# SwitchHead attention: scores with the keys in four partition groups, probabilities turned by VectorE instead of TensorE, row maxima combined through DRAM

## What is computed

```python
def _gate(x, Wsel):                       # sigmoid scores, all but the best two of eight set to zero
    ...
q = _rope(jnp.einsum('bsd,hdp->bhsp', x, Wq))
k = _rope(jnp.einsum('bsd,hdp->bhsp', x, Wk))
v = jnp.einsum('bsd,bhse,hedp->bhsp', x, _gate(x, Wsel_v), Wv)
att = jax.nn.softmax(jnp.einsum('bhsp,bhtp->bhst', q, k) / np.sqrt(P), axis=-1)
o = jnp.einsum('bhst,bhtp->bhsp', att, v)
return jnp.einsum('bhsp,bhse,hepd->bsd', o, _gate(x, Wsel_o), Wo)
```

## Time and profile before

| | |
|---|---|
| runs | 5350.47, 5362.56, 5364.59 us (median 5362.56) |
| the profiled execution | 5350.9 us, of which the span of the trace is 5349.1 us |
| the stage of SwitchHead's loop | 1057 to 3644 us, 2587 us, 256 tiles |
| TensorE in that stage | 2551.35 us busy, granted clock 1.00 |
| VectorE, ScalarE, GpSimd there | 1520.72, 1338.64, 1157.34 us busy |
| DMA there | 0.31 of 16 engines, 81 GB/s |

### The profile page before, as it was taken

How to read it: one execution, slowest core, us unless ns; L and a number is a source line. 1 busy time by engine, 2 the same in 40 slices (tenths; PEclk the granted TensorE clock), 3 DMA queues, 4 the chain that set the end, 5 groups by cost and what they waited for, 6 DMA issues and landing times.

```text
span 5349.1 us, 83763 instructions
## 1 busy us (share of the span) xinstructions
PE 4801.0 (90%) x30340; PEld 2480.0 (46%) x30378; DVE 3571.9 (67%) x4077; ACT 2898.9 (54%) x3797; POOL 2348.7 (44%) x1499
## 2 busy tenths in 40 slices
PE   6989898689999999999999999997888988888856
PEld 2334333256556666565666556564333322222226
DVE  5899999866655565556655674654776778888721
ACT  5665556245445545555455554553555557667743
POOL 4888888535534543535534444443221221120014
PEclk8999999899999999999999999998999999999978
DMA  4555555323332332333323332233112101101005
GB/s 152 189 182 183 179 190 193 124 56 82 86 80 78 86 94 72 82 83 79 94 68 86 89 95 65 72 91 85 39 34 43 41 25 26 25 25 25 2 30 169
DMA packets 202377, 467.59 MB, mean 87 GB/s; under 512 B 35179, under 2 KB 52078, under 8 KB 201316
## 3 DMA queue, kind: packets, MB, share of 16 engines
q1 hardware_dynamic: 198968, 455.89, 29.9%
q0 software_dynamic: 3008, 6.32, 0.3%
HBM read 417.51 MB, written 33.99 MB: 84 GB/s over the span
## 4 chain that ended last, share of the span: by engine, by line
PE 72%; issue 9%; DVE 8%; ACT 6%; POOL 3%; DMA 0%; SPq 0%; POOLq 0%; DVEq 0%; ACTq 0%
PE ps L2258 8%; PE ps L1350 8%; PE ps L1370 8%; PE ps L1389 8%; PE ps L1358 7%; PE ps L1339 7%; PE ps L548 4%; PE ps L2229 3%; PE ps L2211 3%; ACT n_P L2293 3%; PE ps L495 2%; PE ps L1332 2%; DVE ps L713 1%; DVE n_MX L2372 1%; DVE m_HH L734 1%
## 5 line engine op out<-in xcount | busy, mean ns | idle before, releaser
L2372 DVE TENSOR_REDUCE n_MX<-ps 128x2 f32<-128x1024 f32 (+6 forms) x1034 | 982.2, 979 | 235.6 <-PE ps L2211 137.1
L1496 ACT ACTIVATE s_P<-ps,s_MX 128x1024 f32<-128x1024 f32 x512 | 570.4, 1114 | 968.1 <-DVE s_MX L1660 968.0
L2293 ACT ACTIVATE n_P<-ps 128x1024 f32<-128x1024 f32 (+4 forms) x1022 | 825.3, 838 | 447.2 <-PE ps L2229 233.7
L1652 DVE TENSOR_TENSOR XTB<-ps,s_GVJ 128x1024 f32<-128x1024 f32 x256 | 313.2, 1223 | 837.3 <-PE ps L1339 836.4
L771 POOL TENSOR_TENSOR m_PR<-m_HH,m_CS 128x1024 f32<-128x1024 f32 x256 | 605.9, 2381 | 156.2 <-issue 129.4
L1660 DVE TENSOR_REDUCE s_MX<-ps 128x1 f32<-128x1024 f32 x512 | 600.3, 1214 | 32.1 <-PE ps L1350 32.0
L1867 POOL TENSOR_TENSOR s_OG<-s_OG,s_OT 128x1024 f32<-128x1024 f32 x256 | 604.4, 2374 | 38.8 <-DMA s_OG<-s_gt 38.6
L1505 ACT ACTIVATE shared<-ps 128x1024 f32<-128x1024 f32 x512 | 496.7, 1023 | 140.0 <-PE ps L1358 138.4
L1350 PE MATMUL ps<-s_QF 64*128 64x512 f32 x2048 | 510.6, 617 | 28.1 <-POOL s_QF L1859 20.0
L1358 PEld LDWEIGHTS ps<-ident,s_P 128*128 128x128 f32 x4096 | 464.0, 141 | 150.5 <-issue 135.3
L1370 PEld LDWEIGHTS ps<-shared,s_V 128*64 128x64 f32 x8192 | 442.0, 137 | 197.4 <-issue 172.4
(11 more groups left out here) (352 smaller groups left out, 6484.7 us busy)
## 6 DMA issues: line engine op xcount, KB each, us to landing
m_CS<-m_rows_c SPq DMA_DIRECT2D x256, 512.0 KB
s_OG<-s_gt SPq DMA_DIRECT2D x512, 256.0 KB, 4.2
m_BS<-m_rows_c SPq DMA_DIRECT2D x80, 512.0 KB
s_WV<-in_s_v SPq DMA_DIRECT2D x32, 512.0 KB, 4.0
s_TA<-XTB SPq DMA_DIRECT2D x256, 64.0 KB, 2.3
s_WO<-in_s_o SPq DMA_DIRECT2D x32, 512.0 KB, 5.3
g_WB<-in_g_wx SPq DMA_DIRECT2D x23, 578.0 KB
n_parts<-n_PT SPq DMA_DIRECT2D x14, 768.0 KB, 3.4
```

The costliest lines, as they stand in the source:

```text
L2293: ins = s.activation(P[:, at:at + x.shape[1], lo:512], x[:, :, lo:512], ACT.Exp, scale=scale)
L2372: ins = v.tensor_reduce(self.MX[:, q, at:at + x.shape[1], hp, t], x[:, :, 0:width], AX.X, ALU.max)
```

## The change

- `row`: the same products in 32 small matmuls per tile instead of 4. Each takes 32 queries (a), one quarter of the keys (x: of every 128 keys, 32) and one head (h), and writes 32 partitions x 256 columns. The scores of a query now lie in four groups of 32 partitions. ScalarE only copies them to P (`row`).
- `turn`: VectorE transposes P in blocks of 32 x 32 from SBUF to SBUF, one instruction of 128 x 1024 per head. TensorE's 16 transposes and ScalarE's two copies of them are gone. `values` reads PT in another pattern, with the same number and size of matmuls.
- the maximum: VectorE reduces each head of P to four columns (`max`), SyncE writes these 128 x 8 values to DRAM (`max`) and reads them back as 32 x 4 x 8 (`join`); VectorE reduces over the four (`most`), SyncE writes the 32 x 8 result four times (`most`) and reads it back on 128 partitions (`bias`). ScalarE's exponential then runs in place on P, in four pieces of 256 columns per head (`exp`).
- the sums go the same way once per four tiles: write, read (`gather`), reduce, reciprocal and a 32 x 32 transpose on VectorE, write (`spread`), two reads that broadcast over 64 partitions each (`over`). TensorE's four transposes, ScalarE's copy and GpSimd's spreading are gone.
- `v`: the sum over the 8 experts moves from VectorE's one reduction to three additions on GpSimd, of 512, 256 and 128 elements.
- `swap`: the four DMAs of `qk` are issued in the turn after it.
- the order inside `turn`, and six buffers of P instead of four.

```diff
-    NP = 4
+    NP = 6
...
+        k, half = m % 4, lambda late: self.of_half((m - late) // 4)
+        if due(1):
+            out.append(("most", *tile(1)))
         if due(2):
-            g = m - 2
-            out.append(("values", *self.pair(g // 8), g % 8))
-            if g % 4 == 3:
-                out.extend([("keep", *self.of_half(g // 4)), ("sums", *self.of_half(g // 4))])
+            out.append(("turn", *tile(2), 1))
+        if k == 1 and due(5):
+            out.append(("sums", *half(5)))
+        if k == 2 and due(6):
+            out.append(("over", *half(6)))
+        if due(1):
+            out.append(("bias", *tile(1)))
+        if k == 1 and due(5):
+            out.append(("gather", *half(5)))
+        if d in (3, 5) and b < NB and m // 8 + 1 < 8 * NB:
+            out.append(("swap", *self.pair(m // 8 + 1), d // 2 - 1))
         if m < 7:
             next(ahead)
         if due(self.GATED):
@@ -969,18 +989,33 @@
         if due(self.GATED + 1):
             h, e = part(self.GATED + 1)
             out.append(("onto", *self.of_half(h), e))
-            if e == 3:
-                out.append(("collect", *self.of_half(h)))
+        if due(0):
+            out.append(("max", *tile(0)))
+        for _ in range(2 if m == 2 else 1):
+            next(vs, None)
+        if due(1):
+            out.extend([("exp", *tile(1), 0), ("exp", *tile(1), 1)])
+        if k == 1 and due(5):
+            out.append(("recip", *half(5)))
+        if due(1):
+            out.append(("turn", *tile(1), 0))
+        if due(0):
+            out.append(("join", *tile(0)))
+        if k == 1 and due(5):
+            out.append(("spread", *half(5)))
+        if k == 2 and due(6):
+            out.append(("scale", *half(6)))
+        if due(self.GATED + 1) and part(self.GATED + 1)[1] == 3:
+            out.append(("collect", *self.of_half(part(self.GATED + 1)[0])))
+        if due(2):
+            g = m - 2
+            out.append(("values", *self.pair(g // 8), g % 8))
+            if g % 4 == 3:
+                out.append(("keep", *self.of_half(g // 4)))
         if d in (3, 5) and b < NB and m // 8 + 1 < 8 * NB:
             out.append(("rope", *self.pair(m // 8 + 1), d // 2 - 1))
-        next(turns, None)
-        next(turns, None)
         if m < N:
             next(ahead, None)
-        if m % 4 == 0 and due(4):
-            out.append(("recip", *self.of_half(m // 4 - 1)))
-        for _ in range(2 if m == 2 else 1):
-            next(vs, None)
...
+            elif kind == "max":
+                g = self.tile(*step[1:])
+                sp.wait_ge(self.mx_done, g + 1)
+                if g > 1:
+                    sp.wait_ge(self.mg_in, 16 * (g - 1))
+                sp.dma_start(self.mx_d[g % 2], self.MX[:, g % 2, :]).then_inc(self.mx_out, 16)
+            elif kind == "join":
+                g = self.tile(*step[1:])
+                sp.wait_ge(self.mx_out, 16 * (g + 1))
+                if g > 1:
+                    sp.wait_ge(self.most_done, g - 1)
+                sp.dma_start(self.MG[:, g % 2, :, :], self.mx_d[g % 2].rearrange("(x p) e -> p x e", x=4)).then_inc(self.mg_in, 16)
+            elif kind == "most":
+                g = self.tile(*step[1:])
+                sp.wait_ge(self.most_done, g + 1)
+                if g > 1:
+                    sp.wait_ge(self.mb_in, 16 * (g - 1))
+                sp.dma_start(self.mr_d[g % 2].rearrange("(x p) e -> p x e", x=4),
+                             self.MR[:, g % 2, :].unsqueeze(1).to_broadcast([32, 4, 8])).then_inc(self.mr_out, 16)
+            elif kind == "bias":
+                g = self.tile(*step[1:])
+                sp.wait_ge(self.mr_out, 16 * (g + 1))
+                if g > 1:
+                    sp.wait_ge(self.exp_done, 2 * (g - 1))
+                sp.dma_start(self.MB[:, g % 2, :], self.mr_d[g % 2]).then_inc(self.mb_in, 16)
+            elif kind == "sums":
+                k = self.half(*step[1:])
+                sp.wait_ge(self.exp_done, 8 * (k + 1))
+                if k > 1:
+                    sp.wait_ge(self.su_in, 16 * (k - 1))
+                sp.dma_start(self.su_d[k % 2], self.SU[:, k % 2, :]).then_inc(self.su_out, 16)
...
+                rows = self.sums_d[k % 2].rearrange("(t h a) q -> h t (a q)", t=4, h=2)
+                for h in range(2):
+                    sp.dma_start(self.OR[k % 2][64 * h:64 * h + 64, 1, :].rearrange("p (t n) -> p t n", t=4),
+                                 rows[h].partition_broadcast(64)).then_inc(self.or_in, 16)
...
-            elif kind == "qk":
-                k = n(*step)
+            elif kind == "swap":
+                k = n("qk", *step[1:])
                 sp.wait_ge(self.raw_done, k)
                 if k > 1:
                     sp.wait_ge(self.rope_done, k - 1)
...
-                for q in chunks(L):
-                    for h in range(2):
-                        hs = slice(64 * h, 64 * h + 64)
-                        ins = pe.matmul(r.ap(two[h])[:, q], QF[hs, 0, t * 128:(t + 1) * 128], QF[hs, 1, q], start=True, stop=True)
-                        if q.stop == L:
...
+                for a in range(4):
+                    for x in range(4):
+                        for h in range(2):
+                            hs, at = slice(64 * h, 64 * h + 64), 128 * t + 32 * a
+                            keys = QF[hs, 1, :].rearrange("p (k x n) -> p k x n", x=4, n=32)[:, :, x, :]
+                            place = r.ap(two[h])[32 * x:32 * x + 32, 256 * a:256 * a + 256]
+                            ins = pe.matmul(place.rearrange("p (k n) -> p k n", n=32), QF[hs, 0, at:at + 32], keys,
+                                            start=True, stop=True)
+                            if a == x == 3:
...
+                        place = self.O[64 * h:64 * h + 64, 128 * (g % 4):128 * (g % 4) + 128].rearrange("p (a n) -> p a n", n=32)
+                        P = self.PT[g % 2][:, h, :].rearrange("p (a k n) -> p a k n", a=4, n=32)[:, :, i, :]
+                        ins = pe.matmul(place, self.V[j % 2][:, h, i, :], P, start=i == 0, stop=i == NT - 1)
...
-                    s.wait_ge(self.values_done, g - 1)
-                s.activation(self.PT[g % 2][:, step[4], :, :].rearrange("p k n -> p (k n)"), ps, ACT.Copy).then_inc(*r.take(step))
+                    s.wait_ge(self.pt_done, x - self.NP + 1)
+                s.activation(self.P[x % self.NP][:, :], ps, ACT.Copy).then_inc(*r.take(step))
...
+            elif kind == "exp":
+                g, x, h = self.tile(*step[1:4]), self.head(step), step[4]
+                if h == 0:
+                    s.wait_ge(self.mb_in, 16 * (g + 1))
+                    if g % 4 == 0 and g >= 8:
+                        s.wait_ge(self.su_out, 16 * (g // 4 - 1))
+                for a in range(4):
+                    P, at = self.P[x % self.NP][:, 256 * a:256 * a + 256], 8 * (g % 4) + 4 * h + a
+                    ins = s.activation(P, P, ACT.Exp, bias=self.MB[:, g % 2, 4 * h + a:4 * h + a + 1],
+                                       accum_out=self.SU[:, g // 4 % 2, at:at + 1])
...
-                r.taken(v, step)
-                v.tensor_reduce(self.V[u][:, :, t, :], four(self.VP), AX.X, ALU.add).then_inc(self.v_done, 1)
-            elif kind == "row":
-                x = self.head(step)
-                r.filled(v, step)
-                if x >= 8:
-                    r.taken(v, self.old("row", x - 8))
-                v.tensor_reduce(self.MX[:, x % 8:x % 8 + 1], ps, AX.X, ALU.max, negate=True).then_inc(self.mx_done, 1)
+            elif kind == "max":
+                g = self.tile(*step[1:])
+                if g > 1:
+                    v.wait_ge(self.mx_out, 16 * (g - 1))
+                for h in range(2):
+                    x = self.head((*step, h))
+                    r.taken(v, ("row", *step[1:], h))
+                    ins = v.tensor_reduce(self.MX[:, g % 2, 4 * h:4 * h + 4],
+                                          self.P[x % self.NP][:, :].rearrange("p (a k) -> p a k", a=4), AX.X, ALU.max)
+                ins.then_inc(self.mx_done, 1)
+            elif kind == "most":
+                g = self.tile(*step[1:])
+                v.wait_ge(self.mg_in, 16 * (g + 1))
+                if g > 1:
+                    v.wait_ge(self.mr_out, 16 * (g - 1))
+                v.tensor_reduce(self.MR[:, g % 2, :], self.MG[:, g % 2, :, :].rearrange("p x e -> p e x"), AX.X, ALU.max,
+                                negate=True).then_inc(self.most_done, 1)
+            elif kind == "turn":
+                g, x = self.tile(*step[1:4]), self.head(step)
+                v.wait_ge(self.exp_done, x + 1)
+                if g == 0:
+                    v.wait_ge(self.top_done, 1)
+                elif g > 1:
+                    v.wait_ge(self.values_done, g - 1)
+                v.transpose(self.PT[g % 2][:, step[4], :], self.P[x % self.NP][:, :]).then_inc(self.pt_done, 1)
...
+                v.wait_ge(self.su_in, 16 * (k + 1))
```

(19 more changed lines are left out.)

124 lines of the change are left out of this document (52 added, 72 removed).

## The result

The changed kernel takes 5517.42 us, the median of 4 runs (5514.19 to 5529.69), against 5357.18 us for the kernel before on the same chip (4 runs, 5350.47 to 5364.59): a ratio of 1.030, 95% interval 1.028 to 1.033. It is 160 us slower. The forecast was 5275 us, faster; 5517 lies inside the range over all cases (5090 to 5590), but outside that of the forecast (5145 to 5325) and on the other side of no change.

The account below looks back on a forecast made before the run. TensorE bounds the kernel at 10.11 us a turn; after the change three chains and TensorE meet at 8.2, plus (2 x 2.4 + 2 x 1.1 + 0.8)/8 + 0.6 gives 9.8, 5275 us; forecast range 5145 to 5325, all cases 5090 to 5590.

Parts of the forecast that it names:

- rival D: VectorE's transpose runs like the scan, 2.29 us: 10.9 us a turn, 5555 us; chance 0.09.
- rival E: TensorE's eight score regions don't overlap, scores 4.6 us: 10.5 us a turn, 5450 us; chance 0.05.
- Rival C: Small DMAs land slower than alone, 5.0 us per write and read: 11.0 us a turn, 5580 us; chance 0.25.
- a pair: One small DMA write to DRAM and its read back, taken at 1.7 + 2.1 = 3.8 us.
- chain 1: From `most` through its write and read, first head's exponential and transpose, and `collect` to the next `most`: 8.15 us.
- the gates' load is issued right before `most`'s write, which queues behind its tail: 0.4: On SyncE's queue, the write of the joined maxima delayed by 0.4 us of a possible 1.5.
- plain turns: Loop turns without the `qk` or `swap` disturbances, forecast at 8.2 us; wrong if already above 9 us.
- `qk`: In 2 turns of 8, ScalarE's copy behind the exponentials delays VectorE's product and the next `most`: +2.4 us, 10.6 us.
- `swap`: In the turn after `qk`, SyncE's four issues (2.51 us) delay the maxima's write: +1.1 us.
- weights: Loads of 512 KB, one of them between the maxima's write and read: +0.8 us per eight turns.
- `ahead`: half falls into the holes: Pieces of `ahead`, 0.6 us on VectorE and 0.5 on ScalarE per turn, half of it hidden: +0.6 us a turn.
- Chain 3: Over two turns, eight exponentials, copies, last maximum, two DMA round trips, `most` and other work: 16.3 us, 8.15 a turn.

Follow-up runs that it names:

- e1_local: Changed kernel without the maxima's round trips: each partition's own maximum goes straight into its exponentials, four DMAs per tile and `most` gone (result not the reference's): 5022.03 us.
- e3_thin: Changed kernel with the gates' loads cut to 32 of 512 columns after the first three, same number of DMAs (result not the reference's): 5382.75 us.
- e8_thin_qk: Changed kernel with gates' loads cut to a sixteenth of their columns and the `qk` steps ahead of the exponentials (gated output not the reference's): 5315.79 us.
- e12: Changed kernel with `most` moved to the end of the turn before, ahead of the gates' load, `bias` staying where it is: 5609.21 us.
- e14: Changed kernel with `most` and `bias` both moved ahead of the piece of `ahead`, the `qk` steps and the gates' load: 5643.12 us.
- e10: Changed kernel with the two DMAs of the gates' load issued by ScalarE on its own queue instead of SyncE, same place in the list: 5514.84 us.
- e4_lag: Changed kernel with the exponentials and all that follows them one turn later, same work and DMAs: 5333.36 us.
- e6_lag_order: e4_lag with the small steps reordered, among them `qk` ahead of the exponentials, `swap` behind `join`, second head's transpose ahead of `most`: 5222.54 us, ratio 0.976.

## Why the prediction was wrong

**What held.** Only the loop's stage changed. The transpose takes 1231 ns (1.2 taken), so rival D fell; the Trainium skill ("Vector Engine (DVE) Microarchitecture Reference", The reshape front-end and per-opcode configuration), by which it is one element per cycle and lane, agrees. TensorE's scores take 1.96 us in the timeline and 526.8/255 = 2.07 on average against 2.3 taken, so rival E fell: eight regions do run side by side. A piece of the exponential takes 0.495 us (0.52 taken); the estimate of 0.40 by the Trainium skill ("VectorE: DVE Perf Modes", The TRN2 errata) isn't seen in any run here. TensorE alone needs 8.3 us of the turn in e1_local (8.2); after the change it is busy for 2252 us in the stage, at a clock of 0.93, where about 2100 was called for. The forecast called for TensorE's idle time ahead of `values` and ScalarE's ahead of the exponentials: both are there.

**Rival C held in half.** It priced a pair at 5.0 us where I took 3.8, and put its threshold at 4.1. The pair of `most` and `bias` takes 2.8 + 1.6 = 4.4, the pair of `max` and `join` 1.5 + 1.6 = 3.1. The sum of both, 7.5, is what I took for both, 7.6; by the means it is 8.3. So the landings were under-priced by 0.7 us in four at most, and by the medians not at all; they are unevenly spread, and the late one stands in chain 1, where every turn waits for it. Small DMAs do land as alone, except behind the gates. The Trainium skill ("DMA: Bandwidth & Descriptors", Anatomy of one DMA) gives a fixed 2.0 us per DMA; that section is on DMAs that GpSimd issues, while these are SyncE's, and the runs show medians of 1.4 to 1.7 us for them clear of the gates' load.

**The step that failed** is the sentence "the gates' load is issued right before `most`'s write, which queues behind its tail: 0.4". Chain 1 was the right chain, and this term of it was too small. The plain turns (0, 1, 6 and 7) show it best, as they have neither `qk` nor `swap`:

| plain turns, means | forecast | after |
|---|---|---|
| `most` to issue of its write | 0.2 | 0.48 |
| to issue of the read | 2.2 | 2.77 |
| to the first exponential | 2.1 | 2.04 |
| to the end of the first transpose | 3.6 | 3.80 |
| to the next `most` | 0.8 | 0.95 |
| sum | 8.9 | 10.0 |

The 2.2 is 1.7, 0.4 for the gates and 0.1 for weights; the 0.8 is 0.17 for `collect` and 0.6 for the pieces.

Of the 1.1 us that are missing, 0.3 is the write held behind the issues of the gates, for which nothing stood in the sum, and 0.6 is its landing: 2.75 us on average where 1.7 + 0.4 was taken. In the turns of `qk` the landing is later still, 3.4 us. The remainder is the transpose and what VectorE does behind it. "`ahead`: half falls into the holes" was not the fault: 0.95 us lie between the transpose and the next `most`, and 0.8 was taken.

Chain 3 was mis-sized as well, but it isn't what made most turns late. It measures 19.4 us over two turns, 9.7 a turn, and not 8.15. The maxima end 2.65 us after the copies and not 1.2, as VectorE has both of them to take there (2.1 us) and often a transpose before (0.5); their write waits 0.9 us on SyncE, 0.4 of it behind the issues of `swap`; and the trip of `most` is 5.1 and not 4.0. Yet it has 1.9 us of slack on average. In the whole stage VectorE waits 109 us for MG, in 69 turns, 0.4 us a turn. Of the 66 of these within tiles 10 to 252, 44 (81 us) are tiles whose maxima left SyncE right behind the four issues of `swap`: the delay that the forecast had priced at 1.1 us. In plain turns it waits 0.2 us on average.

**By kinds of turn.** I had 8.2 plus 0.7 for every turn (0.6 for pieces, 0.1 for weights): 8.9 for a plain one, 11.3 for `qk`, 10.0 for `swap`. Measured from `most` to `most`: 10.2, 10.1, 10.6 and 9.2 for turns 0, 1, 6 and 7, on average 10.0; 12.6 and 12.4 for `qk`; 10.1 and 10.0 for `swap`. A plain turn is 1.1 above, the condition that the prediction named as making it wrong, and `qk` 1.2 above; together (4 x 1.1 + 2 x 1.2)/8 = 0.85 us a turn, which is the whole difference between the 10.65 of the table and 9.8. The turns of `swap` come out as forecast in their terms too: there the write leaves 0.2 us after `most` and lands in 2.1 us (2.1 taken), and VectorE waits 1.3 us for MG (1.1 taken). Where the landing is as taken, the sum holds.

**What the runs show in its place.** The order of one list closes a loop through the engines and four DMAs, chain 1 fills the turn, and a late landing in it is paid in every turn. e1_local: without the trips a turn would have gone from 10.11 to 8.8 us, 1.3 saved; the trips cost 1.93, which is more. e3_thin and e8_thin_qk: queueing behind the bytes of the gates (0.53 us a turn) and `qk` (0.28) are real and add. e12 moves the queueing to the read, which is in chain 1 too; e14 moves it to the tile's maxima, and uses up the slack of the chains through `join` and more; e10 spreads it over all of them. e4_lag and e6_lag_order: giving the exponentials one turn more and putting the steps in the order in which their inputs arrive takes 184 and 295 us off. The forecast's time was within reach with this work, not with this order.

**Left open.** What ScalarE pays for issuing the gates in e10_gates_act (0.66 us for each of the two) was not separated from the delays that moved. Nor was what TensorE's lower clock adds to the stage's 163 us: in e1_local it came back to 0.98 with the trips gone, so it goes with the waiting, but no run holds it fixed. e3_thin shows what the gates' bytes cost; what their two issues cost by holding the write (0.24 us a turn in the table) is read from the traces alone, as no run took the issues away and left the rest.

## What to carry to other kernels

Before a latency is put into a software pipeline, write down every chain that returns to its own start, also those over two turns, with each engine's queue order in them, and add the disturbances to each; a chain that "meets" the turn without slack was late here. A round trip through DRAM, 3.1 to 4.4 us here, is better given a turn of slack in the pipeline from the start (here 184 us for one turn more), and no bulk transfer right ahead of it, in its own queue or another. Before a late step is moved, ask what will then leave directly behind the bulk load. And compare means as well as medians: a median of 1.4 us hid that the delay had only gone elsewhere.

## What the runs showed of the hardware

- A DMA of 4 KB lands in 1.4 to 1.7 us at the median clear of the gates' load, out of SBUF or out of DRAM (after, e10). Issued next behind 512 KB on the same queue it takes 2.8 to 3.4 us at the median, whichever of the small DMAs it is (after, e12, e14); behind 32 KB in the same number of DMAs, 1.6 (e3_thin).
- Another queue doesn't spare it that: within 1 us after the start of an issue of gates, 4 KB took 3.6 us on the same queue (after) and 3.4 to 3.9 with the gates on ScalarE's queue (e10).
- Issues of small DMAs take SyncE 0.32 to 0.38 us at the median (after); the two of the gates 1.2 us, and 2.17 in the turn shown. An issue behind them is held for that time.
- 64 matmuls of 256 columns in eight regions of 64 x 32 take 1.96 us in the turn shown, no more than the same work in two regions of 64 x 128 took (1.99).
- ScalarE in place on SBUF with bias and accumulation: pieces of 256 columns start 0.49 us apart.
- TensorE's granted clock, a mean over the stage between its levels of 2.4 GHz (1.00) and 1.2 GHz (0.50), was 1.00 before, where TensorE hardly waited, 0.93 after the change, where its weight loads waited for transposes 157 times (295.8 us), and 0.98 in e1_local, where they did so 39 times (69.1 us).
